# Projecting the values of two turns at once in every second step of a hand-pipelined transformer kernel

## The reference

```python
x = x + attn_a(layernorm(x))   # 16 heads of 8, biases on q, k, v, two scores masked to -1e9
x = x + ffn(layernorm(x))      # top 2 of 8 experts for each item, 128 -> 64 -> 128, gelu
x = x + attn_b(layernorm(x))   # 16 heads of 8, one w_qkv, scores divided by sqrt(128)
x = x + ffn(layernorm(x))      # the same experts' weights again

# attention, for each item
q, k, v = (n @ Wq, n @ Wk, n @ Wv)                   # each 256 x 128, in 16 heads of 8
out = softmax(q @ k.T * scale) @ v @ Wo
```

## Time and profile before

| | us |
|---|---|
| median of 3 timed runs | 963.03 |
| lowest and highest of them | 961.36, 967.95 |
| the profiled execution | 963.5 |
| its span, first to last instruction | 961.7 |
| busy time of PE, DVE, ACT, POOL | 859.7, 778.5, 765.7, 666.3 |

### The profile page before, as it was taken

How to read it: one execution, slowest core, us unless ns; L and a number is a source line. 1 busy time by engine, 2 the same in 40 slices (tenths; PEclk the granted TensorE clock), 3 DMA queues, 4 the chain that set the end, 5 groups by cost and what they waited for, 6 DMA issues and landing times.

```text
span 961.7 us, 33578 instructions
## 1 busy us (share of the span) xinstructions
PE 859.7 (89%) x13102; PEld 492.3 (51%) x13102; DVE 778.5 (81%) x1394; ACT 765.7 (80%) x1299; POOL 666.3 (69%) x1280
## 2 busy tenths in 40 slices
PE   2579999999999999999999999999999988988875
PEld 1235555555555555555555555555555544554543
DVE  1679999999998889888898989988878968869533
ACT  2168888888888888988888888988888877877863
POOL 8456777767886868868686877868777777654442
PEclk9689999999999999999999999999999999999986
DMA  6577555545544445435444454535445444344001
GB/s 184 156 216 221 156 158 172 159 140 157 157 154 126 127 145 143 146 111 151 135 146 136 137 154 126 147 122 157 125 125 165 120 139 127 109 133 135 4 24 45
DMA packets 144717, 132.04 MB, mean 137 GB/s; under 512 B 9616, under 2 KB 127536, under 8 KB 144432
## 3 DMA queue, kind: packets, MB, share of 16 engines
q1 hardware_dynamic: 143456, 128.49, 45.4%
q10 hardware_dynamic: 1104, 1.41, 0.5%
HBM read 73.76 MB, written 55.57 MB: 134 GB/s over the span
## 4 chain that ended last, share of the span: by engine, by line
PE 53%; POOL 13%; DVE 11%; ACT 9%; issue 7%; DMA 3%; SPq 1%; POOLq 1%; ACTq 1%; DVEq 0%
PE values_bank L779 16%; PE ring L808 9%; PE ring L794 8%; DVE nmax L601 8%; PE m_bank L907 5%; ACT probs L672 5%; PE ring L845 3%; PE m_bank L932 3%; PE m_bank L973 3%; POOL xy L492 2%; PE values_bank L920 2%; ACT hT L735 2%; POOL rest L508 1%; DMA q_stack<-maxT 1%; PE m_bank L946 1%
## 5 line engine op out<-in xcount | busy, mean ns | idle before, releaser
L601 DVE TENSOR_REDUCE nmax<-ring 128x4 f32<-128x1024 f32 x512 | 608.1, 1215 | 113.0 <-PE ring L794 109.5
L672 ACT ACTIVATE probs<-ring 128x1024 f32<-128x1024 f32 x512 | 512.1, 1026 | 92.3 <-PE ring L808 78.4
L779 PE MATMUL values_bank<-probs,values 128*32 128x256 f32 x4096 | 276.6, 384 | 0.7 <-ACT probs L672 0.7
L794 PE MATMUL ring<-k_stack,q_stack 64*128 64x256 bf16 x2048 | 191.4, 275 | 38.3 <-ACT probs L672 22.9
L492 POOL TENSOR_SCALAR xy<-x,mv,rstd 128x128 f32<-128x128 f32 x256 | 200.6, 793 | 7.9
L808 PE MATMUL ring<-q_stack,k_stack 64*128 64x256 bf16 x2048 | 180.1, 273 | 13.8 <-DVE nmax L601 8.2
L779 PEld LDWEIGHTS values_bank<-probs,values 128*32 128x32 f32 x4096 | 121.3, 109 | 61.4 <-issue 21.7
L808 PEld LDWEIGHTS ring<-q_stack,k_stack 64*128 64x128 bf16 x2048 | 78.0, 94 | 114.9 <-issue 54.7
L794 PEld LDWEIGHTS ring<-k_stack,q_stack 64*128 64x128 bf16 x2048 | 79.3, 95 | 111.0 <-ACT probs L672 42.4
L416 POOL TENSOR_SCALAR mparts<-nmax 128x32 bf16<-128x32 f32 x64 | 13.9, 217 | 164.8 <-DVE nmax L601 164.3
L508 POOL TENSOR_TENSOR rest<-qk,parts 128x512 f32<-128x512 f32 x64 | 74.2, 1159 | 5.4
(11 more groups left out here) (102 smaller groups left out, 1041.2 us busy)
## 6 DMA issues: line engine op xcount, KB each, us to landing
q_stack<-scratch SPq DMA_DIRECT2D x128, 256.0 KB
k_stack<-scratch SPq DMA_DIRECT2D x128, 256.0 KB
scratch<-parts SPq DMA_DIRECT2D x128, 192.0 KB, 2.2
scratch<-parts SPq DMA_DIRECT2D x128, 128.0 KB, 2.2
scratch<-parts SPq DMA_DIRECT2D x128, 64.0 KB, 2.4
out<-x SPq DMA_DIRECT2D x16, 256.0 KB, 2.6
x<-in_x SPq DMA_DIRECT2D x3, 768.0 KB, 6.7
q_stack<-maxT SPq DMA_DIRECT2D x128, 12.0 KB
```

Of the source, the lines that this page charges most:

```text
L601: nc.vector.tensor_reduce(dst, src, axis=AX.X, op=ALU.max, negate=True).then_inc(max_done, 1)
L672: nc.scalar.activation(probs[g % 2][:, c:c + 2, :, :], pair_of("exps", n, p)[:, :, :].rearrange("p x (k q) -> p x k q", k=TILES), ACT.Exp) ...
L779: last = nc.tensor.matmul(values_bank[32 * c:32 * (c + 1), a * TOKENS:(a + 1) * TOKENS], values[turn % RING][:, k, PER_GROUP * g + c, :], ...
L794: last = nc.tensor.matmul(pair_of("scores", turn, p)[:, a, t * TOKENS:(t + 1) * TOKENS], q_stack[z][rows, p, t * P:(t + 1) * P], k_stack[z ...
```

## The change

The value projection is made only in odd steps, for turns n + 3 and n + 4 together: 16 matmuls instead of 8, filling the whole of `values_bank`. It waits for `xnT` of turn n + 4, as the projection of q and k just ahead does. ACT copies the bank out in odd steps only, again in two instructions, each now twice as wide (256 elements of each partition, before 128). The values have six buffers (`VRING`) in place of four (`RING`), in one tensor. POOL has six pairs of opening memsets in place of four. The scratch for dynamic DMAs goes to 4096 bytes. In the first `weigh` of an even step the wait for the copies of the same step is gone.

```diff
--- before.py
+++ after.py
@@ -33,6 +33,7 @@
 EARLY_LOADS, CONSTANTS = 3, 8
 CHUNKS = ((0, 2), (2, 9), (9, 15), (15, 21), (21, 27), (27, ITEMS))
 RING = 4
+VRING = 6
 TURNS = 2 * ITEMS
 GROUP = 4
 DEEP = 2 * GROUP
@@ -71,7 +72,7 @@
 
         q_stack = [sb(f"q_stack{r}", [P, PAIRS, TOKENS], BF16) for r in range(RING)]
         k_stack = [sb(f"k_stack{r}", [P, PAIRS, TOKENS], BF16) for r in range(RING)]
-        values = [sb(f"values{r}", [P, TILES, HEADS, 32]) for r in range(RING)]
+        values = sb("values", [P, VRING, TILES, HEADS, 32])
         qk32 = [sb(f"qk32_{i}", [P, 2, TOKENS]) for i in range(2)]
         rest = [sb(f"rest{i}", [P, 2, TOKENS]) for i in range(2)]
         parts = [sb(f"parts{i}", [P, 3, 2, TOKENS], BF16) for i in range(2)]
@@ -143,9 +144,10 @@
                     dst = D[ALL_SLOTS * qk + SLOTS:ALL_SLOTS * (qk + 1)]
                     sp.dma_start(dst, tail_c[m, qk]).then_inc(tail_in, 16)
 
-        def of_group(r, g):
-
-            return values[r][:, :, :, :].rearrange("p t (b c) w -> p (t b) c w", c=PER_GROUP)[:, g::IN_SHARE]
+        def of_group(r, count, g):
+
+            some = values[:, r:r + count, :, :, :].rearrange("p r t (b c) w -> p (r t b) c w", c=PER_GROUP)
+            return some[:, g::IN_SHARE]
 
         ring = [ctx.enter_context(nc.psum_tensor(f"ring{i}", [P, 2, 512], FP32)) for i in range(3)]
         values_bank = ctx.enter_context(nc.psum_tensor("values_bank", [P, 512], FP32))
@@ -164,7 +166,7 @@
         consts_in = sem("consts_in")
         x_in = [sem(f"x_in{c}") for c in range(len(CHUNKS))]
         set_up, early_in, weights_ready = sem("set_up"), sem("early_in"), sem("weights_ready")
-        HALF_SET, VALUES_SET, ALL_SET = 1, 1 + RING + 1, 1 + RING + 2
+        HALF_SET, VALUES_SET, ALL_SET = 1, 1 + VRING + 1, 1 + VRING + 2
 
         def load_x(sp, c):
 
@@ -196,13 +198,13 @@
 
         def gpsimd_opening(pool):
             nc.gpsimd.memset(minus_half[:, :, :], -0.5).then_inc(set_up, 1)
-            for r in range(RING):
-                nc.gpsimd.memset(values[r][:, :, :, :], 0.0).then_inc(set_up, 1)
-            for r in range(RING):
+            for r in range(VRING):
+                nc.gpsimd.memset(values[:, r, :, :, :], 0.0).then_inc(set_up, 1)
+            for r in range(VRING):
                 pool.wait_ge(set_up, HALF_SET + r + 1)
                 for g in range(IN_SHARE):
                     at = SUMS * g + HEAD
-                    last = nc.gpsimd.memset(of_group(r, g)[:, :, :, at:at + 1], 1.0)
+                    last = nc.gpsimd.memset(of_group(r, 1, g)[:, :, :, at:at + 1], 1.0)
             last.then_inc(set_up, 1)
             nc.gpsimd.memset(wide[:, :, :], 0.0)
             nc.gpsimd.memset(hot[:, :, :], 0.0)
@@ -710,15 +712,15 @@
                         else:
                             last = nc.scalar.copy(qk32[i][:, :, :], src)
                         last.then_inc(qk32_ready, 1)
-                    if p == 1 and live(n + 3):
-
-                        act.wait_ge(v_done, (n + 3) + 1)
+                    if p == 1 and n % 2 and live(n + 3):
+
+                        act.wait_ge(v_done, (n + 3) // 2 + 1)
                         act.wait_ge(set_up, VALUES_SET)
-                        if live(n - 1):
-                            act.wait_ge(pv_done, (n - 1) * GROUPS + GROUPS)
-                        src = values_bank[:, 0:TOKENS].rearrange("p (b c d) -> p b c d", c=PER_GROUP, d=HEAD)
+                        if live(n - 2):
+                            act.wait_ge(pv_done, (n - 2) * GROUPS + GROUPS)
+                        src = values_bank[:, :].rearrange("p (b c d) -> p b c d", c=PER_GROUP, d=HEAD)
                         for g in range(IN_SHARE):
-                            last = nc.scalar.copy(of_group((n + 3) % RING, g)[:, :, :, SUMS * g:SUMS * g + HEAD], src[:, g::IN_SHARE])
+                            last = nc.scalar.copy(of_group((n + 3) % VRING, 2, g)[:, :, :, SUMS * g:SUMS * g + HEAD], src[:, g::IN_SHARE])
                         last.then_inc(v_ready, 1)
                     if p == 3 and group_at(n) is not None:
 
@@ -768,16 +770,16 @@
 
                     pe.wait_ge(exp_done, turn * PAIRS + PER_GROUP // 2 * (g + 1))
                     if g == 0:
-                        pe.wait_ge(v_ready, turn + 1)
+                        pe.wait_ge(v_ready, turn // 2 + 1)
                         if turn > 0:
                             pe.wait_ge(oT_ready, (turn - 1) + 1)
-                        if live(turn + 3):
-                            pe.wait_ge(v_ready, (turn + 3) + 1)
+                        if turn % 2 and live(turn + 3):
+                            pe.wait_ge(v_ready, (turn + 3) // 2 + 1)
                     a, g2 = divmod(g, IN_SHARE)
                     for k in range(TILES):
                         for c in range(PER_GROUP):
                             last = nc.tensor.matmul(values_bank[32 * c:32 * (c + 1), a * TOKENS:(a + 1) * TOKENS],
-                                                    values[turn % RING][:, k, PER_GROUP * g + c, :], probs[g % 2][:, c, k, :],
+                                                    values[:, turn % VRING, k, PER_GROUP * g + c, :], probs[g % 2][:, c, k, :],
                                                     start=(g2 == 0 and k == 0), stop=(g2 == IN_SHARE - 1 and k == TILES - 1),
                                                     skip_group_check=True)
                     last.then_inc(pv_done, 1)
@@ -907,18 +909,20 @@
                                 last = nc.tensor.matmul(m_bank[cols, a * TOKENS:(a + 1) * TOKENS], wmat[:, cols], xnT[(n + 4) % 2][:, :],
                                                         start=(a == 0), stop=(a == 1), skip_group_check=True)
                         last.then_inc(qk_done, 1)
-                    if p == 2 and live(n + 3):
-                        wv = projections[(n + 3) // ITEMS][2]
-                        if live(n + 2):
-                            pe.wait_ge(v_ready, (n + 2) + 1)
+                    if p == 2 and n % 2 and live(n + 3):
+                        if live(n + 1):
+                            pe.wait_ge(v_ready, (n + 1) // 2 + 1)
                         if live(n - 1):
                             pe.wait_ge(oT_ready, (n - 1) + 1)
-                        pe.wait_ge(xnT_ready, (n + 3) + 1)
-                        for t in range(TILES):
-                            for cols in QUARTERS:
-                                at = slice(t * P + cols.start, t * P + cols.stop)
-                                last = nc.tensor.matmul(values_bank[cols, t * P:(t + 1) * P], xnT[(n + 3) % 2][:, at], wv,
-                                                        start=(t == 0), stop=(t == TILES - 1), skip_group_check=True)
+                        pe.wait_ge(xnT_ready, (n + 4) + 1)
+                        wv = projections[(n + 3) // ITEMS][2]
+                        for j in range(2):
+                            for t in range(TILES):
+                                to = slice((j * TILES + t) * P, (j * TILES + t + 1) * P)
+                                for cols in QUARTERS:
+                                    at = slice(t * P + cols.start, t * P + cols.stop)
+                                    last = nc.tensor.matmul(values_bank[cols, to], xnT[(n + 3 + j) % 2][:, at], wv,
+                                                            start=(j == 0 and t == 0), stop=(j == 1 and t == TILES - 1), skip_group_check=True)
                         last.then_inc(v_done, 1)
                     if p == 3 and live(n):
                         exp_side(n, 2)
@@ -1019,7 +1023,7 @@
         "pick": np.tile(np.eye(ITEMS), (3, 1)).astype(ml_dtypes.bfloat16),
     }
     arrays = {f"in_{k}": np.ascontiguousarray(v) for k, v in arrays.items()}
-    nc = bacc.Bacc("TRN2", target_bir_lowering=False, num_devices=1)
+    nc = bacc.Bacc("TRN2", target_bir_lowering=False, num_devices=1, dynamic_dma_scratch_size=4096)
     args = [nc.dram_tensor(k, v.shape, mybir.dt.from_np(v.dtype), kind="ExternalInput").ap() for k, v in arrays.items()]
     out = nc.dram_tensor("out", (ITEMS, TOKENS, WIDTH), FP32, kind="ExternalOutput").ap()
     build(nc, *args, out)
```

## The result

| | before | after |
|---|---|---|
| device time, median of 5 runs | 962.58 us (960.55 to 967.95) | 970.54 us (968.18 to 972.97) |
| span of the profiled execution | 961.7 us | 971.2 us |

The ratio is 1.0076, with a 95% interval from 1.0046 to 1.0107: slower by 0.8%, inside the 1% that I had set as "within". The forecast was 973.1 us, its own range 969.5 to 976, the wide one 962 to 976.5. The medians differ by 8.0 us, the two profiled executions by 9.5; the forecast was +10.1.

What follows compares the result with a forecast made beforehand. Two loops of 12.2 us, PE's own and one through DVE, were taken to bound the kernel. 11.2 - 0.6 - 0.8 + 0.35 = 10.1 us on 963.0 gave 973.1 us, own range 969.5 to 976, wide 962 to 976.5.

Steps and rivals of the forecast that it cites:

- PE's way and DVE's way of the same length: Ordinary steps: PE's own loop and one through DVE's maxima and e7 both take 12.2 us, within about 0.01 us.
- Odd steps, +0.43 each: Odd ordinary steps: the added matmuls delay s3 and all behind it; 26 x 0.43 = 11.2 us over steps 1 to 51.
- Ordinary even steps, 0: Even ordinary steps: s3 comes earlier, but DVE holds PE at e7, so they stay at 12.21 us; gain 0.
- about 0.4 us of idle before e7: Sign in the profile after: in even steps PE idles some 0.4 us before e7, released by DVE's maxima.
- the 0.3 that were named: Sign in the profile after: in odd steps DVE idles about 0.3 us before the maxima of s3.
- Even steps that do gain, -0.6: Steps 22, 30, 38 and 46, where extra transposes make s3 late and DVE idles 0.14 us: -0.6 us together.
- The opening, +1.2: Before step 0: POOL's two more buffer fills delay PE's first transposes; the opening's chain moves 1.2 us, bounds 0 and 2.0.
- The -0.85 of step 0: Step 0, an even one: the projection on the chain there falls away, -0.85 us.
- Step 53 to the end, -0.8: Last steps: odd 55 and 59 +0.43 each, even 54, 56 and 58 together -1.68, 53 and 57 0; sum -0.8 us.
- The halves cancel: Rival: even steps give back 0.44 us, so the 11.2 go to about 0; 962 to 963.5 us; chance 0.20.
- ACT's saved instructions count: Rival: ACT is the bound and its fewer copies gain 3 to 9 us; 954 to 960 us; chance 0.06.
- Slower than the forecast: Rival: in odd steps ACT's wider copies hold the first `weigh` or the exponential of e2; 976 to 982 us; chance 0.12.

Runs made afterwards that it cites:

- 7: Kernel before, with DVE's statistics and aggregate of turn n - 2 moved behind the maxima of s7: 964.44 us, ratio 1.0011.
- 8: Kernel before, with PE's second `weigh` group split in two halves, e5 and s6 between them: 962.89 us, ratio 0.9988.
- 5: Kernel before with the moves of 7 and 8 together: 960.26 us, ratio 0.9966.
- 9: Kernel before with the moves of 7 and 8, and DVE's aggregate of turn n + 6 also behind the maxima of s7: 954.85 us, ratio 0.9892.
- 1: Kernel before, with DVE's row maxima for p = 3 taken over the first 128 keys only: 967.28 us, ratio 0.9997.
- 3: Kernel before, with DVE's row maxima for p = 0 and p = 3 taken over the first 128 keys only: 964.85 us, ratio 0.9997.

## Why the prediction came out right

**PE's way and DVE's way of the same length: right at e7, and shown there; read too wide for the rest.** Each edit alone gives nothing (7 and 8); with both the kernel is faster (5 and 9). But DVE's loop isn't the unbroken row from s0 to s6: 0.5 and 1.1 us less ahead of s4 change nothing (1 and 3), and what binds is the stretch from s4 to e7. No run shortens that stretch alone. The 53 waits of the earlier trace rows were no evidence for it: 44 are at e5, and the list still has 54 and 52 in experiments 1 and 3. And PE waited at a second place besides s7, the transposes of the maxima's parts, for 0.13 us behind POOL.

**Odd steps, +0.43 each: right.** 12.64 us for 12.21, and +10.6 for 25 of them; the 26th, step 1, gave +0.31.

**Ordinary even steps, 0: right in size (-0.03), incomplete in mechanism.** The prediction said that DVE holds PE at e7 for the whole 0.44. It does so for 0.11. Another 0.12 is lost at e3, which the prediction didn't see, and 0.17 at s3 to an exponential of ACT, which isn't DVE's doing at all. The forecast of about 0.4 us of idle before e7 therefore failed, while the length of the step held. In odd steps DVE idles 0.25 us before the maxima of s3, near the 0.3 that were named.

**Even steps that do gain, -0.6: mis-sized**, measured -3.4 for all even steps from 4 to 52. The step that failed is that only steps with extra transposes gain, 0.14 each. It looked at DVE's idle time only; PE's waits for POOL in the same steps (0.67 us in step 30) weren't read, and the later arrival of PE takes 0.40 us out of such a wait. Six further steps (12, 20, 28, 36, 44, 52) give 0.15 each, -0.9 together. The -0.63 of step 26 and the +0.48 of step 16 are for the most part landings and not the change.

**The opening, +1.2: mis-sized**, measured +2.4 to e0 of step 0. The part that the change makes was right, 1.26 us at the first transposes. The rest lies in DMA landings. Of the same code e0 of step 0 started at 52.57 and 55.27 us in two executions (the kernel before; experiment 1, which differs from it in nothing up to there but the maxima). Over the seven traces with four fills in front (some with DVE's or PE's order changed) it starts at 52.57 to 55.27, 53.8 on average, and over the five with six fills at 54.95 to 56.22, 55.6 on average: an estimate of 1.7 us for the change, with some tenths of scatter. The -0.85 of step 0 was too large: that step is 0.41 us shorter.

**Step 53 to the end, -0.8: mis-sized**, measured 0.0. Single steps went from -2.3 (58) to +1.5 (59): the bursts hand their delays to each other, and adding up rows of the chain doesn't tell that. No run separates them.

The errors of +1.2, -2.8 and +0.8 us, with +0.3 in steps 0 to 2 and -0.2 in the odd ones, nearly cancel. The 10.1 of the forecast against 9.5 in the spans is closer than its terms, and that is luck; the large term, the odd steps, is not.

**The rivals.** *The halves cancel:* refuted, even steps stayed at 12.18. It isn't right with DVE lightened either (1.0055). *ACT's saved instructions count:* refuted. The copies take 0.68 us in their row, and the exponential behind them starts 172.43 - 171.85 = 0.58 us after them, near the 0.50 that I set for two; the median copy is 0.39 us; 64 instructions fewer took 2.0 us off ACT's 765.7. The Trainium skill, "ScalarE: Activation LUTs", section "Rules for kernel authors", states its 0.3 us for an ACTIVATE whose bias is a pointer operand. Put on each of the 64 it would give an estimate of 19; this trace doesn't agree. *Slower than the forecast:* did not come about; PE's first `weigh` of the odd step starts at 173.06 by the timeline, and both copies are over at 172.53.

## What to carry to other kernels

When an engine idles in one short place of a step and another engine's result arrives just as it is needed, compute both ways before moving anything, and for each place where something starts right behind a foreign result: a piece of work taken from one step and put into the next costs its full length there and may save none here. An edit that shortens one of two equal ways measures as nothing, and that isn't a reason to drop it; try it together with one for the other way. A count of waits isn't yet evidence of a hold: look at which place they stand, and whether they outlast the idle time that is usual there. Small work of an engine that others wait for belongs into the place where that engine idles anyway, behind the last result that someone waits for.

## What was unexpected in the hardware

Landings of the small DMAs into `q_stack` vary from execution to execution: PE waited for them 5.5 us in 3 places before the change, 11.8 us in 10 in experiment 1, 9.4 us in 6 in experiment 9. Steps 0, 27 and 54 are among them in all three, the others change. One longer landing in the opening shifts everything by 1 us, about as much as the fills did.

A projection of one turn's values, 16 matmuls in the trace, costs 0.44 us when it is added behind others of its kind (1.88 us from the projection's start to s3, for 1.44). Sixteen fp32 matmuls with 256 columns are followed by further fp32 ones after 154.97 - 154.09 = 0.88 us, but by the bf16 scores only after 1.00 us. The value projection shows the same 0.12: it is 0.56 us to s3 where 0.44 are its own.
